# Delta rule of a vision tower: the dot sums on TensorE, keys scaled later, no zeroed state, and the keys' roots by one GpSimd power a group

## The reference, cut to what matters

```python
def _L1_attn_ref(x, Wq, Wk, Wv, Wo, Wbet, Wf, norm_w):
    q = jax.nn.silu(x @ Wq).reshape(b, n, h, hd)
    k = jax.nn.silu(x @ Wk).reshape(b, n, h, hd)
    k = k * jax.lax.rsqrt(jnp.sum(k * k, -1, keepdims=True) + 1e-12)
    v = (x @ Wv).reshape(b, n, h, hd)
    beta = 2.0 * jax.nn.sigmoid(x @ Wbet)
    a = jax.nn.sigmoid(x @ Wf)

    def step(S, inp):
        qt, kt, vt, at, bt = inp
        Sd = at[..., None, None] * S
        u = vt - jnp.einsum('bhk,bhkv->bhv', kt, Sd)
        Sn = Sd + bt[..., None, None] * kt[..., None] * u[:, :, None, :]
        o = jnp.einsum('bhk,bhkv->bhv', qt, Sn)
        return (Sn, o)
    S0 = jnp.zeros((b, h, hd, hd), x.dtype)
    _, o = jax.lax.scan(step, S0, (tfirst(q), tfirst(k), tfirst(v), tfirst(a), tfirst(beta)))
    ...
```

## Time and profile before

| | |
|---|---|
| median of three runs | 1323.74 us (1318.02 to 1327.02) |
| the profiled execution | 1322.82 us |
| its span, first to last instruction | 1320.8 us |
| busy: PE, DVE, ACT, POOL | 88%, 59%, 40%, 35% of the span |
| mean granted TensorE clock | 0.951 of full |
| key preparation of the four groups on VectorE | 607.4 to 658.6 us |
| the loop's 64 tokens, first to last L1856 | 660.3 to 892.4 us |

### The profile page before, as it was taken

How to read it: one execution, slowest core, us unless ns; L and a number is a source line. 1 busy time by engine, 2 the same in 40 slices (tenths; PEclk the granted TensorE clock), 3 DMA queues, 4 the chain that set the end, 5 groups by cost and what they waited for, 6 DMA issues and landing times. The chain is left out here.

```text
span 1320.8 us, 25953 instructions
## 1 busy us (share of the span) xinstructions
PE 1163.5 (88%) x9667; PEld 927.6 (70%) x9667; DVE 781.4 (59%) x1721; ACT 528.2 (40%) x1318; POOL 465.8 (35%) x635
## 2 busy tenths in 40 slices
PE   6999998498999999989279999995899999879975
PEld 4666667388999999984047777774677777667653
DVE  3666665511122212267989999995577777533687
ACT  3455453111221122126256666562334444335455
POOL 0111111223233333244378777772212122101556
PEclk9999999699999999999689999998999999999985
DMA  4111100589888888559400000002000040018611
GB/s 144 46 39 43 49 10 17 214 322 390 311 328 314 326 327 325 184 147 260 127 1 0 2 1 1 2 1 79 13 14 10 10 169 32 2 38 305 199 49 65
DMA packets 82716, 162.31 MB, mean 123 GB/s; under 512 B 42976, under 2 KB 61536, under 8 KB 76576
## 3 DMA queue, kind: packets, MB, share of 16 engines
q1 hardware_dynamic: 63776, 114.44, 25.3%
q0 software_dynamic: 10224, 44.05, 8.7%
q10 hardware_dynamic: 8592, 2.16, 0.7%
HBM read 134.28 MB, written 26.35 MB: 122 GB/s over the span
## 5 line engine op out<-in xcount | busy, mean ns | idle before, releaser
L936 PE MATMUL banks<-rowsT,w_up 128*128 128x128 f32 x1716 | 199.5, 276 | 0.2 <-DMA w_up<-in_up_w 0.2
L936 PEld LDWEIGHTS banks<-rowsT,w_up 128*128 128x128 f32 x1716 | 196.3, 193 | 0.5 <-DMA w_up<-in_up_w 0.4
L1467 PE MATMUL banks<-xT_d,ident 128*128 128x512 f32 x256 | 124.4, 609 | 30.0 <-POOL xT_d L1930 26.6
L1477 PEld LDWEIGHTS banks<-chain_q,ident 128*128 128x128 f32 x992 | 120.5, 188 | 29.2 <-issue 29.2
L1611 ACT ACTIVATE banks<-banks,rate 128x256 f32<-128x256 f32 x252 | 98.3, 447 | 82.7 <-DVE made L1823 81.4
L1930 POOL TENSOR_TENSOR xT_d<-kb,ys 128x1024 f32<-128x1024 f32 x64 | 123.7, 1932 | 1.3 <-DVE ys L1856 1.3
L1477 PE MATMUL banks<-chain_q,ident 128*128 128x128 f32 x992 | 120.9, 273 | 0.0
L1105 DVE TENSOR_TENSOR hT<-banks,silu 64x128 f32<-64x128 f32 x39 | 11.0, 283 | 167.5 <-ACT silu L993 167.5
L950 PE MATMUL banks<-w_down,hT 128*128 128x256 f32 x468 | 107.5, 379 | 0.6 <-DVE res L1115 0.6
L950 PEld LDWEIGHTS banks<-w_down,hT 128*128 128x128 f32 x468 | 85.9, 190 | 11.0 <-issue 1.0
L1467 PEld LDWEIGHTS banks<-xT_d,ident 128*128 128x128 f32 x256 | 44.0, 192 | 66.2 <-POOL xT_d L1930 27.5
(11 more groups left out here) (330 smaller groups left out, 2396.6 us busy)
## 6 DMA issues: line engine op xcount, KB each, us to landing
w_up<-in_up_w SPq DMA_DIRECT2D x39, 1408.0 KB, 5.8
w_down<-in_down_w POOLq DMA_DIRECT2D x39, 768.0 KB, 4.9
inter<-res_x SPq DMA_DIRECT2D x16, 512.0 KB, 3.3
back<-inter SPq DMA_DIRECT2D x15, 512.0 KB, 3.9
patches<-in_patches SPq DMA_DIRECT2D x16, 384.0 KB, 3.3
f<-in_f SPq DMA_DIRECT2D x6, 1024.0 KB, 11.7
ys<-token_rows SPq DMA_DIRECT2D x16, 256.0 KB, 2.8
xn_rows<-xn_all SPq DMA_DIRECT2D x16, 128.0 KB, 1.7
```

The costliest lines, as they stand in the source:

```text
L936: ins = pe.matmul(out[:, m * P:(m + 1) * P], w[:, c, m * P:(m + 1) * P], x[:, c, :], start=(c == 0), stop=(c == 1))
L1467: pe.matmul(S[t % 2][:, halves[h], :, :], ident[:, :], outer[t % 2][:, halves[h], :, :], start=False, stop=True, skip_group_check=True).th ...
L1477: ins = pe.matmul(o_sum[n % 2].rearrange("p (n s) -> p n s", s=2), ident[:, :], products[:, n % 2, :, k, :], start=(k == 0), stop=(k == HD ...
```

## The change

The change edits only this layer. In the order of the program:

- **Sums of neighbours' products.** GpSimd's products go to a buffer for each group: the first to a free part of `ys`, the others into `o`, where group g takes the place of the squares of group g-1, once these are summed (`keys_summed`). TensorE sums the 16 components with the identity matrix into bank 4, 16 matmuls of 63 columns a group (`sum_dots`), behind all projections. VectorE multiplies `link` of all groups by the sums in one operation, in group 3 between the factors and `ka`, and counts `linked`.
- **Roots.** VectorE only sums and guards the squares; GpSimd raises them to -0.5 in one operation on 128x64 (`norm_keys`), and VectorE waits for that (`keys_normed`).
- **`kb` later.** `kb_scale` is now counted by the last of VectorE's small operations on factors, and VectorE waits for it itself before `ka`.
- **No zero state.** ScalarE copies v(0) to u(0) (`first_correction`); the first outer product is written to PSUM with start=True; VectorE makes u(1) from two columns of `prod`; its products of states begin with token 2. Counts in the waits of `read_keys`, `fade`, `copy_last_group` and others move by one or two.
- **GpSimd's queue.** A product of neighbours and the power stand ahead of the loads of v of group 1 and of q of group 1, and the load of q of group 2 ahead of `kb` of that group. Its zeroing goes. Ahead of the loop it waits for `linked` and for v(1) in place.

```diff
+    first_dots = rows_flat[:, n_copy + n_u:n_copy + n_u + HD * TOK].rearrange("p (d t) -> p d t", d=HD)
+    dots = [first_dots] + [o[:, g, :, :] for g in range(CG - 1)]
+    dot_sums = banks[:, 4, 0:CG * TOK].rearrange("p (g t) -> p g t", g=CG)
...
+        def sum_dots(g):
+            pe.wait_ge(sem("neighbours"), g + 1)
+            for d in range(HD):
+                ins = pe.matmul(dot_sums[:, g, 1:], ident[:, :], dots[g][:, d, 1:], start=(d == 0), stop=(d == HD - 1))
+            ins.then_inc(sem("dots_summed"), 1)
...
+            pe.matmul(S[t % 2][:, halves[h], :, :], ident[:, :], outer[t % 2][:, halves[h], :, :], start=(t == 0),
...
-        pe.wait_ge(sem("zeroed"), 1)
+        pe.wait_ge(sem("made2"), CG)
+        for g in range(CG):
+            sum_dots(g)
         pe.wait_ge(sem("rate_made"), CG)
-        pe.wait_ge(sem("made0"), CG)
-        pe.wait_ge(sem("made1"), CG)
-        for b in (1, 0):
-            for h in range(2):
-                ins = pe.matmul(banks[:, 2 * b + h, :], ident[:, :], zeros, start=True, stop=True)
-                if b == 0:
-                    ins.then_inc(sem(f"state{h}"), 1)
...
+        def first_correction():
+            act.copy(u[0], v[:, :, :, 0]).then_inc(sem("first_u"), 1)
...
+        first_correction()
         for m in range(6):
             act.wait_ge(sem(f"stored{m}"), 16 * CG)
-        place_values(0)
         place_values(1)
...
         def sum_keys(g):
             dve.wait_ge(sem("k_squared"), g + 1)
-            once.mark(dve.tensor_reduce(n2[:, g, :], o[:, g, :, :].rearrange("p d t -> p t d"), AX.X, ALU.add))
-            once.settle()
-            once.mark(dve.tensor_scalar(n2[:, g, :], n2[:, g, :], 1e-12, None, ALU.add))
-            once.settle()
-            x, y = n2[:, g, :].bitcast(I32), rn[:, g, :].bitcast(I32)
-            once.mark(dve.tensor_scalar(y, x, 1, None, ALU.logical_shift_right))
-            once.settle()
-            once.mark(dve.tensor_scalar(y, y, -1.0, float(0x5F3759DF), ALU.mult, ALU.add))
-            once.settle()
-            for _ in range(3):
-                newton(n2[:, g, :], rn[:, g, :], tmp[:, g, :])
+            dve.tensor_reduce(n2[:, g, :], o[:, g, :, :].rearrange("p d t -> p t d"), AX.X, ALU.add
+                              ).then_inc(sem("keys_summed"), 1)
+            dve.wait_ge(sem("keys_summed"), g + 1)
+            dve.tensor_scalar(n2[:, g, :], n2[:, g, :], 1e-12, None, ALU.add).then_inc(sem("keys_guarded"), 1)
...
         def scale_keys(g):
             dve.wait_ge(sem(f"rates{g}"), 16)
+            once.mark(dve.tensor_scalar(rate[:, g, 1, :], rate[:, g, 1, :], 0.5, 0.5, ALU.mult, ALU.add))
             if g >= 2:
                 dve.wait_ge(sem("kb_made"), g - 1)
+            dve.wait_ge(sem("keys_normed"), g + 1)
             by_rate, by_rn = f[:, 0, g % 2, :], f[:, 1, g % 2, :]
-            dve.scalar_tensor_tensor(out=by_rn, in0=rate[:, g, 0, :], scalar=1.0, in1=rn[:, g, :],
-                                     op0=ALU.add, op1=ALU.mult).then_inc(sem("kb_scale"), 1)
-            once.mark(dve.tensor_scalar(rate[:, g, 1, :], rate[:, g, 1, :], 0.5, 0.5, ALU.mult, ALU.add))
+            once.mark(dve.scalar_tensor_tensor(out=by_rn, in0=rate[:, g, 0, :], scalar=1.0, in1=rn[:, g, :],
+                                               op0=ALU.add, op1=ALU.mult))
...
             once.settle()
-            once.mark(dve.tensor_tensor(by_rate[:, 1:], by_rate[:, 1:], rate[:, g, 1, 0:TOK - 1], ALU.mult))
-            once.settle()
+            dve.tensor_tensor(by_rate[:, 1:], by_rate[:, 1:], rate[:, g, 1, 0:TOK - 1], ALU.mult
+                              ).then_inc(sem("kb_scale"), 1)
+
+        def make_ka(g):
+            dve.wait_ge(sem("kb_scale"), g + 1)
             once.mark(dve.tensor_tensor(ka[:, :, g, :].rearrange("p t d -> p d t"), k[:, g, :, :],
-                                        bcast(by_rate, 1, HD), ALU.mult))
...
-        def link_keys(g):
-            dve.wait_ge(sem("neighbours"), g + 1)
...
-            once.mark(dve.tensor_tensor(link[:, g, 1:], link[:, g, 1:], n2[:, g, 1:], ALU.mult))
+                                        bcast(f[:, 0, g % 2, :], 1, HD), ALU.mult))
...
         for g in range(CG):
             sum_keys(g)
             scale_keys(g)
-            link_keys(g)
+            if g == CG - 1:
+                dve.wait_ge(sem("dots_summed"), CG)
+                dve.tensor_tensor(link[:, :, 1:], link[:, :, 1:], dot_sums[:, :, 1:], ALU.mult).then_inc(sem("linked"), 1)
+            make_ka(g)
...
-        for m in range(6):
-            dve.wait_ge(sem(f"stored{m}"), 16 * CG)
-        once.mark(dve.memset(prod[0][:, :, :, HD], 0.0))
-        once.settle()
...
-        for t in range(TOK):
+        dve.wait_ge(sem("values_placed"), 1)
+        dve.wait_ge(sem("corrected"), 1)
+        dve.tensor_reduce(u[1], prod[1][:, :, :, HD:ROW], AX.X, ALU.add).then_inc(sem("u_made"), 1)
+        for t in range(2, TOK):
...
             for h in range(2):
-                dve.wait_ge(sem(f"prod_made{h}"), t + 1)
-            dve.wait_ge(sem("values_placed"), t + 1)
-            if t:
-                dve.wait_ge(sem("corrected"), t)
-            if t >= 2:
-                dve.wait_ge(sem("outer_made"), t - 1)
+                dve.wait_ge(sem(f"prod_made{h}"), t - 1)
+            dve.wait_ge(sem("values_placed"), t)
+            dve.wait_ge(sem("corrected"), t)
+            dve.wait_ge(sem("outer_made"), t - 1)
             dve.tensor_reduce(u[t % 2], prod[t % 2], AX.X, ALU.add).then_inc(sem("u_made"), 1)
...
         def multiply_neighbours(g):
             pool.wait_ge(sem(f"chain_k{g}"), 16)
             if g:
-                pool.wait_ge(sem("dots_summed"), g)
-            pool.tensor_tensor(dots, k[:, g, :, 1:], k[:, g, :, 0:TOK - 1], ALU.mult).then_inc(sem("neighbours"), 1)
+                pool.wait_ge(sem("keys_summed"), g)
+            pool.tensor_tensor(dots[g][:, :, 1:], k[:, g, :, 1:], k[:, g, :, 0:TOK - 1], ALU.mult
+                               ).then_inc(sem("neighbours"), 1)
+
+        def norm_keys(g):
+            pool.wait_ge(sem("keys_guarded"), g + 1)
+            pool.tensor_tensor(rn[:, g, :], n2[:, g, :], minus_half[:, 0:1].to_broadcast([P, TOK]), ALU.pow
+                               ).then_inc(sem("keys_normed"), 1)
...
-        pool.memset(zeros, 0.0).then_inc(sem("zeroed"), 1)
         pool.memset(small[:, :], 1e-6).then_inc(sem("small_set"), 1)
         prepare(pool)
         load_chain(pool, 0, "v", v)
         load_chain(pool, 0, "q", q)
+        multiply_neighbours(0)
+        norm_keys(0)
         load_chain(pool, 1, "v", v)
-        multiply_neighbours(0)
         scale_keys(0)
         multiply_neighbours(1)
+        norm_keys(1)
         load_chain(pool, 1, "q", q)
         scale_keys(1)
         load_chain(pool, 2, "v", v)
         multiply_neighbours(2)
+        norm_keys(2)
+        load_chain(pool, 2, "q", q)
         scale_keys(2)
-        load_chain(pool, 2, "q", q)
         multiply_neighbours(3)
+        norm_keys(3)
         scale_keys(3)
         pool.wait_ge(sem("kb_made"), CG)
+        pool.wait_ge(sem("linked"), 1)
+        pool.wait_ge(sem("values_placed"), 1)
         for t in range(TOK):
-            pool.wait_ge(sem("u_made"), t + 1)
+            if t == 0:
+                pool.wait_ge(sem("first_u"), 1)
+            else:
+                pool.wait_ge(sem("u_made"), t)
             if t + 1 < TOK:
...
```

More of the change, by code:

```diff
@@ L1292, in delta_layer @@
     w, w_rate, rate_made = (front[n] for n in ("w", "w_rate", "rate_made"))
-    zeros = front["ys"][:, 0, :, :].rearrange("p k d -> p (k d)")
     stats, agg, shift, xT = (front[n] for n in ("stats", "agg", "shift", "xT"))
@@ L1315, in delta_layer @@
     rows_flat = front["ys"][:, :, :, :].rearrange("p n k d -> p (n k d)")
-    n_zero, n_copy = 2 * D, 2 * HD * HD
-    dots = rows_flat[:, n_zero:n_zero + HD * (TOK - 1)].rearrange("p (d t) -> p d t", d=HD)
-    Sc_ring = rows_flat[:, n_zero:n_zero + n_copy].rearrange("p (r v k) -> p r v k", r=2, v=HD)
+    n_copy, n_u = 2 * HD * HD, 2 * CG * HD
+    first_dots = rows_flat[:, n_copy + n_u:n_copy + n_u + HD * TOK].rearrange("p (d t) -> p d t", d=HD)
+    dots = [first_dots] + [o[:, g, :, :] for g in range(CG - 1)]
+    dot_sums = banks[:, 4, 0:CG * TOK].rearrange("p (g t) -> p g t", g=CG)
+    Sc_ring = rows_flat[:, 0:n_copy].rearrange("p (r v k) -> p r v k", r=2, v=HD)
     Sc = [Sc_ring[:, i, :, :] for i in range(2)]
-    u_ring = rows_flat[:, n_zero + n_copy:n_zero + n_copy + 2 * CG * HD].rearrange("p (r g v) -> p r g v", r=2, g=CG)
+    u_ring = rows_flat[:, n_copy:n_copy + n_u].rearrange("p (r g v) -> p r g v", r=2, g=CG)
     u = [u_ring[:, i, :, :] for i in range(2)]
@@ L1466, in add_outer @@
             pe.wait_ge(sem("outer_made"), t + 1)
-            pe.matmul(S[t % 2][:, halves[h], :, :], ident[:, :], outer[t % 2][:, halves[h], :, :], start=False,
```

(34 more changed lines are left out.)

6 lines of the change are left out of this document (1 added, 5 removed).

## The result

The changed kernel took 1348.24 us (median of 4 runs, 1337.20 to 1350.38) against 1322.95 for the kernel before on the same chip: a ratio of 1.016, 95% interval 1.0117 to 1.0203. It is slower, and the forecast of 1306.5 with its range of 1300 to 1340 was wrong. A second set of ten runs of the same changed kernel (e4) gave 1341.01 against 1326.78, ratio 1.010 (1.0068 to 1.0132): slower by 1 to 2%. The profiled execution of the first set took 1348.09, with a span of 1346.4 against 1320.8.

What follows compares the result with a forecast made beforehand. Until the token loop VectorE's own chain, group behind group, bounds the kernel. With TensorE's sums setting the start, the first correction begins at 645.4 instead of 661.75: 1322.8 - 16.4 = about 1306.5 us, range 1300 to 1340.

Steps and rivals of the forecast that it cites:

- GpSimd gains: GpSimd's queue, between product of neighbours and `kb`: one added power of 64 columns per group, taken at up to 1.6 us.
- the bounds: Length of GpSimd's 64-column power: 0.66 us if its extra is paid once, 22.6 us if paid at each column.
- break-even: Length of GpSimd's power from which the change turns against itself: 5.7 us, 90 ns a column.
- the low end: GpSimd's power pays its extra once, 0.66 us; up to 1.6 us taken, TensorE's sums set the start, 1306.5; chance 0.48.
- rival C: GpSimd's power: every column pays what the single one pays, above 8 us each, so the kernel gets slower; chance 0.20.
- high end: GpSimd's power pays the extra 0.35 us at each column: 22.6 us, correction at 729.5, 1390.5 in all.
- 639.1 + 4X: Before the loop: when GpSimd is free for the first correction, four powers in series included, if they set the start.
- the sum of a period: One group from power to power: power, DMA issue, four VectorE steps, `ka`, `kb`, product and hand-overs; 8.0 us besides the power.
- the long part of C: GpSimd's power longer than 10 us, so a time above 1340, outside the range; chance about 0.15.
- the mark: Start of the token loop: GpSimd's first correction, at 661.75 before; what moves it moves the end, forecast 16.4 us earlier.
- TensorE's cover: Before the loop: TensorE's 13.2 us of sums hide GpSimd's 2 to 3 us waits at loads, some 4 us to spare.
- Rival D: TensorE's sums at twice the price, 26.4 us, if it idles and is granted half its clock: 1319.5; chance 0.05.

Runs made afterwards that it cites:

- e3: Changed kernel with GpSimd's power split into one, two, four and eight pieces in groups 0 to 3: 1342.57 us (one run).
- e2: Changed kernel with GpSimd's power replaced by a plain operation writing 1.0, keys not normalised: 1310.69 us, ratio 0.989 against the kernel before.
- e1: Changed kernel with the root back on VectorE instead of GpSimd's power, all else kept: 1315.65 us, ratio 0.9882 against the kernel before.

## Why the prediction was wrong

**The step that failed** is "*GpSimd gains* one power of 64 columns per group, X us", taken at up to 1.6. It took 10.54. It lay within the bounds, 0.66 and 22.6, and beyond the break-even of 5.7; the choice between the bounds failed. (No run has a power between 0.24 and 10.5 us. From the measured 16.4 us and four powers in series the break-even would lie at 10.54 - 16.4 / 4 = 6.4, an estimate.) In place of TensorE's sums, which were to set the start, the four powers set it: the last sums were ready at 667.48, the last power at 670.84. The argument for the low end was that the nearest row has one column and that "nothing shows that the rest isn't fixed too". The row bore the other reading just as well: by e3 a single column is 0.33 + 0.16 = 0.49 us (0.55 in the earlier trace rows), so of the extra over a plain product about half was paid at each column, not once. Between ends that lie a factor of 34 apart, with the break-even inside, a row of one column can't choose, and 0.48 on the low end was too much.

By e3 each column pays 0.16 us, at every width from 8 to 64. The Trainium skill, "GPSIMD Engine Reference", section "Performance pitfalls for Q7 kernels", which the prediction set beside rival C, says that a dependent chain in fp32 pays at each element. The trace agrees that the price is paid at each column; that a dependent chain makes it isn't shown, and the price came to less than half of the high end that the prediction read from it (10.54 against 22.6).

**Rival C, with its formula, is what happened.** For X = 10.54, 639.1 + 4X puts the correction at 681.3, 19.5 later than before, and the time at 1342.3; e4's ten runs give 1341.0. That the two are so near is partly luck: the formula forecasts 19.5 us more than before, and measured are 16.4 in the preparation and 14.2 between e4's medians. The outer product behind it came at 676.13, or 678.4 on the clock of before (keys at 605.13 and not 607.38): the formula is some 3 us too long, most of it because VectorE's four small steps (617.94 to 618.93) run beside GpSimd's DMA issue (617.87 to 618.48), which the sum of a period counted one behind the other.

**The range failed with it.** Its upper end, 1340, was X = 10, and left the long part of C outside.

**What held**, by e2 and the rows after: the place of the mark (the loop is 231.4 to 232.3 us in every version); TensorE at its sums right behind the projections; `ka` first and `kb` at 4.0 behind it in groups 0 to 2, though not in group 3; the correction held by the last `ka`, 1.73; loads in GpSimd's queue costing nothing under TensorE's cover. TensorE's sums were 1.2 us longer than estimated. Rival D's half clock came, and was hidden.

**What the forecast didn't see** is how little the power could have brought. e1 and e2 differ in the whole root, eleven VectorE steps a group, and their preparation by 1.4 us (40.02, 38.65): e2's VectorE, rid of the steps, waits 4.25 us for TensorE's sums, and e1's comes just as they end, with its last `kb` (641.65, 2.37) still ahead of the correction. The gain of this change came from the other edits, 14.6 us in e1: there `kb` later is worth 5.4 us and the sums on TensorE 1.5. The others (no zero state, a buffer for each group's products, the order of GpSimd's queue) weren't taken apart.

## What to carry to other kernels

Before an operation moves to another engine, ask what its removal is worth if it were free at the new place; here that was 1.4 us, against a price that by the bounds could be 4 x 22.6 = 90. Where a sum hangs on an operation that no row shows at its width, the break-even price per column says more than a likely value, and a range has to reach past the price's upper bound as long as no row excludes it. Two elementwise operations that shut each other out can run together when one operand of VectorE's lies in PSUM.
